# Rearranging the last three tiles of a routed decoder layer: one root for two rows, a sum on TensorE, norms on VectorE

## What is computed

```python
logits = x @ Wr + br
probs = softmax(logits)
top_w, top_idx = top_k(probs, 1)
h = silu(x @ Wg[e]) * (x @ Wu[e])      # D_FF = 1024, e = top_idx
y = h @ Wd[e]
x = layernorm(x + y * top_w)           # over the 256 columns, eps = 1e-5
```

## Time and profile before

| what | us |
|---|---|
| median of 3 runs | 197.69 |
| lowest and highest of them | 196.77, 198.11 |
| span of the profiled execution, first to last instruction | 194.3 |
| TensorE busy in it | 176.0 (91%) |
| VectorE busy | 132.0 (68%) |
| ScalarE busy | 103.3 (53%) |
| GpSimd busy | 103.0 (53%) |
| mean granted TensorE clock | 0.980 of full |

### The profile page before, as it was taken

One profiled execution on the slowest core, in us unless ns is written; L12 is line 12 of the kernel. 1 busy time (PEld: TensorE's weight loads), 2 busy tenths in 40 slices (PEclk: granted clock), 3 DMA queues, 4 the chain that ended last, 5 costly groups with the idle time before them and its releaser, 6 DMA issues.

```text
span 194.3 us, 3905 instructions
## 1 busy us (share of the span) xinstructions
PE 176.0 (91%) x969; PEld 140.0 (72%) x969; DVE 132.0 (68%) x406; ACT 103.3 (53%) x274; POOL 103.0 (53%) x130
## 2 busy tenths in 40 slices
PE   1999997999999898989999999999999999999810
PEld 0677775447888655668888788888888888888610
DVE  3269996895678887536554454444799986888950
ACT  3136776725567935537664946643665422455530
POOL 7006356770126884627772168860588810377683
PEclk9999999999999999999999999999999999999975
DMA  5999999246999223146544105444050000011010
GB/s 157 359 336 418 378 366 319 73 139 168 322 334 405 101 85 94 29 130 173 221 149 150 46 0 165 164 162 167 0 162 3 0 0 3 0 57 56 22 62 24
DMA packets 15317, 29.14 MB, mean 150 GB/s; under 512 B 1726, under 2 KB 11968, under 8 KB 15170
## 3 DMA queue, kind: packets, MB, share of 16 engines
q1 hardware_dynamic: 13568, 25.68, 39.4%
q0 software_dynamic: 1440, 3.22, 4.7%
q10 hardware_dynamic: 290, 0.01, 0.1%
HBM read 20.41 MB, written 9.28 MB: 153 GB/s over the span
## 4 chain that ended last, share of the span: by engine, by line
PE 68%; POOL 11%; issue 7%; DMA 5%; DVE 3%; ACT 3%; POOLq 1%; SPq 1%; DVEq 0%; ACTq 0%
PE bank L484 14%; PE bank L486 13%; PE bank L485 13%; POOL out_tokens L473 5%; PE bank L729 4%; PE bank L563 4%; PE bank L652 3%; PE bank L629 3%; POOL rstd L395 3%; DMA arena<-in_attn_w 3%; PE bank L594 2%; PE bank L572 2%; PE bank L511 2%; DMA x_sorted<-buf,slot 1%; PE bank L498 1%
## 5 line engine op out<-in xcount | busy, mean ns | idle before, releaser
L391 POOL TENSOR_TENSOR w_lo<-stage,w_hi 128x512 fp32r<-128x512 f32 x40 | 51.4, 1305 | 44.0 <-ACT w_hi L803 44.0
L912 ACT ACTIVATE gate<-bank 128x256 f32<-128x256 f32 x44 | 17.0, 387 | 48.5 <-PE bank L486 48.5
L1206 DVE TENSOR_TENSOR hid<-bank,gate 128x256 f32<-128x256 f32 x44 | 18.7, 425 | 30.5 <-ACT gate L912 30.2
L484 PE MATMUL bank<-w_hi,xr 128*128 x88 | 35.9, 408 | 1.4 <-DVE xr L1164 0.8
L486 PE MATMUL bank<-w_hi,xr 128*128 x88 | 34.7, 395 | 0.0
L485 PE MATMUL bank<-w_lo,xr 128*128 x88 | 34.7, 394 | 0.0
L484 PE MATMUL bank<-w_hi,hT 128*128 x88 | 28.5, 324 | 0.7 <-DVE hT L1211 0.7
L803 ACT ACTIVATE w_hi<-stage 128x512 fp32r<-128x512 f32 x48 | 28.6, 630 | 0.3 <-PE bank L486 0.3
L486 PE MATMUL bank<-w_hi,hT 128*128 x88 | 24.9, 282 | 0.0
L485 PE MATMUL bank<-w_lo,hT 128*128 x88 | 24.8, 282 | 0.0
L484 PEld LDWEIGHTS bank<-w_hi,xr 128*128 128x128 f32 x88 | 16.6, 189 | 4.4 <-issue 2.3
(11 more groups left out here) (182 smaller groups left out, 329.7 us busy)
## 6 DMA issues: line engine op xcount, KB each, us to landing
stage<-in_w_ffn SPq DMA_DIRECT2D x16, 768.0 KB, 4.5
rows<-x_sorted SPq DMA_DIRECT2D x22, 132.0 KB, 2.3
x_sorted<-padrow SPq DMA_DIRECT2D x1, 2244.0 KB, 10.2
x_sorted<-padrow SPq DMA_DIRECT2D x1, 2112.0 KB, 16.4
buf<-in_x_tok SPq DMA_DIRECT2D x1, 1024.0 KB, 11.0
w_hi<-in_ctx SPq DMA_DIRECT2D x1, 1024.0 KB, 11.5
w_hi<-in_ctxT SPq DMA_DIRECT2D x1, 1024.0 KB, 14.0
x_sorted<-padrow SPq DMA_DIRECT2D x1, 792.0 KB, 12.7
```

What stands on the lines that cost most here:

```text
L391: g.tensor_tensor(out=lo, in0=src, in1=hi.bitcast(F32), op=ALU.subtract).then_inc(split_lo, 1)
L484: mm(dst, xhi, whi, start=start, stop=False)
L912: a(gate[:, (T + j) % 2, :], fA[j % 2][:, 0:FQ], ACT.Silu).then_inc(silu_done, 1)
L1206: v.tensor_tensor(out=hid[:, (T + j) % 2, :], in0=fA[j % 2][:, FQ:2 * FQ], in1=gate[:, (T + j) % 2, :], op=ALU.mult).then_inc(h_done, 1)
```

## The change

At the end of the kernel:

- Tile 10's `acc` is formed in the third quarter as `rows*lsum + acc` in place of `acc*topw + rows`, and its last sum is made by TensorE: an identity matmul puts `acc` into the bank ahead of the down products of item 43. VectorE takes the moments of tile 10 straight from the bank (`finish_last`). Since the row is then larger by the factor `lsum`, the eps added to its variance is `eps*lsum^2`, which one more instruction in `gates` makes (`eps_last`).
- GpSimd takes one root of two columns for tiles 9 and 10 (`last_roots`). It stands behind store 7 and ahead of store 8.
- The norms of tiles 9 and 10 are made by VectorE in one instruction each (`norm_direct`), and no longer by ScalarE.
- In the last steps VectorE makes the low part of item 43 ahead of the moments of tile 8. For tiles 1 to 7 `finish_norm(t-1)` moves from behind the moments of tile t to just ahead of them.

```diff
--- before.py
+++ after.py
@@ -146,6 +146,8 @@
         lexp = sb("lexp", [P, T, E])
         lsum = sb("lsum", [P, T])
         topw = sb("topw", [P, T])
+        eps_last = sb("eps_last", [P, 1])
+        rstd_last = sb("rstd_last", [P, 2])
 
         reach = rows[:, T - 3, 0:CHUNKS * BLOCKS].rearrange("p (c j) -> p c j", c=CHUNKS)
         has_slot = rows[:, T - 2:T, :].rearrange("p t c -> p (t c)")[:, 0:T * BLOCKS].rearrange("p (t j) -> p t j", t=T)
@@ -229,7 +231,7 @@
         mask_ready, r_done, slot_ready = (sem(n) for n in ("mask_ready", "r_done", "slot_ready"))
         tables, row_table = sem("tables"), sem("row_table")
         lexp_done, topw_ready = sem("lexp_done"), sem("topw_ready")
-        out_ready = sem("out_ready")
+        out_ready, last_added = sem("out_ready"), sem("last_added")
 
 
         LN1, LN3 = 0, CHUNKS
@@ -271,6 +273,7 @@
         CONSTS = 23
 
         items = [(q, t) for q in range(NQ) for t in range(T)]
+        LAST, ITEM_LAST = T - 1, NQ * T - 1
         block = ctx.enter_context(nc.Block())
 
 
@@ -465,14 +468,26 @@
                     if q < NQ - 1:
                         for k in quarter_pieces(q + 1, t):
                             split(k)
-            root(LN3, 0, 0)
-            for t in range(T):
-                if t + 1 < T:
-                    root(LN3 + t + 1, (t + 1) % 2, 0)
+            def root_of(t):
+                root(LN3 + t, t % 2, 0)
+
+            def last_roots():
+                pool.wait_ge(var_ready, LN3 + T)
+                g.tensor_tensor(out=rstd_last[:], in0=mv[:, :, 0, 1], in1=mhalf[:, 0:2], op=ALU.pow).then_inc(rstd_ready, 1)
+
+            def store(t):
                 pool.wait_ge(out_ready, t + 1)
                 g.indirect_dma_start(out=out, out_offset=bass.IndirectOffsetOnAxis(ap=outidx[:, t:t + 1], axis=0),
                                      in_=buf[:, t, 0:D], in_offset=None, bounds_check=TOKENS - 1,
                                      oob_is_err=False).then_inc(d_out, 16)
+
+            root_of(0)
+            for t in range(T - 3):
+                root_of(t + 1)
+                store(t)
+            last_roots()
+            for t in range(T - 3, T):
+                store(t)
 
 
         @block.tensor
@@ -731,15 +746,18 @@
 
             def fdown(j):
                 q, t = items[j]
-                pe.wait_ge(hlo_done, j + 1)
                 if j >= 2:
                     pe.wait_ge(y_read, T + j - 1)
                 b = j % 2
                 off = offs.pop(j)
+                if j == ITEM_LAST:
+                    pe.wait_ge(last_added, 1)
+                    mm(fY[j % 2][:, 0:D], ident[:], acc[:, LAST, :], start=True, stop=False)
+                pe.wait_ge(hlo_done, j + 1)
                 for k in range(FQ // P):
                     w = bass.ds(off + ((q % 2) * E * CHUNK + GU + k * D), D)
                     last = split_mm(fY[j % 2][:, 0:D], hT[:, b, 0, k * P:(k + 1) * P], hT[:, b, 1, k * P:(k + 1) * P],
-                                    w_hi[:, w], w_lo[:, w], k == 0, k == FQ // P - 1)
+                                    w_hi[:, w], w_lo[:, w], k == 0 and j != ITEM_LAST, k == FQ // P - 1)
                 last.then_inc(y_done, 1)
 
             pe.wait_ge(tables, 2)
@@ -937,7 +955,7 @@
                     if 1 <= i <= len(items):
                         fhhi(i - 1)
                 t = i - 4 - (len(items) - T)
-                if t >= 0:
+                if 0 <= t < T - 2:
                     norm_row(t)
                 if i < len(items):
                     q, t = items[i]
@@ -1219,7 +1237,11 @@
                 elif q < NQ - 1:
                     v.tensor_tensor(out=acc[:, t, :], in0=fY[j % 2][:, 0:D], in1=acc[:, t, :],
                                     op=ALU.add).then_inc(y_read, 1)
-                if q == NQ - 2:
+                if q == NQ - 2 and t == LAST:
+                    dve.wait_ge(y_read, T + j + 1)
+                    v.scalar_tensor_tensor(out=acc[:, t, :], in0=rows[:, t, 0:D], scalar=lsum[:, t:t + 1],
+                                           in1=acc[:, t, :], op0=ALU.mult, op1=ALU.add).then_inc(last_added, 1)
+                elif q == NQ - 2:
                     dve.wait_ge(y_read, T + j + 1)
                     step(v.scalar_tensor_tensor(out=acc[:, t, :], in0=acc[:, t, :], scalar=topw[:, t:t + 1],
                                                 in1=rows[:, t, 0:D], op0=ALU.mult, op1=ALU.add))
@@ -1228,18 +1250,35 @@
                 dve.wait_ge(lexp_done, 1)
                 step(v.reduce_sum(lsum[:], lexp[:], AX.X))
                 step(v.reciprocal(topw[:], lsum[:]))
+                step(v.scalar_tensor_tensor(out=eps_last[:], in0=lsum[:, LAST:T], scalar=EPS, in1=lsum[:, LAST:T],
+                                            op0=ALU.mult, op1=ALU.mult))
                 step(v.tensor_copy(outidx[:], rows[:, :, TOK]))
 
-            def finish(t):
+            def finish_sum(t):
 
                 dve.wait_ge(y_done, T + len(items) - T + t + 1)
                 r = buf[:, t, 0:D]
                 v.scalar_tensor_tensor(out=r, in0=fY[(len(items) - T + t) % 2][:, 0:D], scalar=topw[:, t:t + 1],
                                        in1=acc[:, t, :], op0=ALU.mult, op1=ALU.add).then_inc(y_read, 1)
+
+            def finish_moments(t):
                 dve.wait_ge(y_read, len(items) + t + 1)
-                step(v.bn_stats(stats[:, t % 2, :], r))
+                step(v.bn_stats(stats[:, t % 2, :], buf[:, t, 0:D]))
                 step(v.bn_aggr(mv[:, t % 2, 0, :], stats[:, t % 2, :]))
                 variance_eps(t % 2, 0).then_inc(var_ready, 1)
+
+            def finish_last():
+                dve.wait_ge(y_done, T + len(items))
+                step(v.bn_stats(stats[:, LAST % 2, :], fY[ITEM_LAST % 2][:, 0:D]))
+                step(v.bn_aggr(mv[:, LAST % 2, 0, :], stats[:, LAST % 2, :]))
+                v.scalar_tensor_tensor(out=mv[:, LAST % 2, 0, 1:2], in0=mv[:, LAST % 2, 0, 1:2], scalar=eps_last[:],
+                                       in1=ones_f[:, 0:1], op0=ALU.add, op1=ALU.mult).then_inc(var_ready, 1)
+
+            def norm_direct(t):
+                r = fY[ITEM_LAST % 2][:, 0:D] if t == LAST else buf[:, t, 0:D]
+                v.scalar_tensor_tensor(out=buf[:, t, 0:D], in0=r, scalar=mv[:, t % 2, 0, 0:1],
+                                       in1=rstd_last[:, t % 2:t % 2 + 1].broadcast_to([P, D]),
+                                       op0=ALU.subtract, op1=ALU.mult).then_inc(out_ready, 1)
 
             def finish_norm(t):
                 dve.wait_ge(rstd_ready, LN3 + t + 1)
@@ -1248,7 +1287,7 @@
                 v.scalar_tensor_tensor(out=nmr[:, t % 2:t % 2 + 1], in0=mv[:, t % 2, 0, 0:1], scalar=-1.0,
                                        in1=rstd[:, t % 2, 0:1], op0=ALU.mult, op1=ALU.mult).then_inc(nmr_ready, 1)
 
-            for i in range(len(items) + 3):
+            for i in range(len(items) + 1):
                 if i == EARLY:
                     fhlo(i - 1)
                     fxlo(i)
@@ -1259,16 +1298,30 @@
                         fxlo(i + 1)
                     if i < len(items):
                         fhidden(i)
+                    if i == len(items):
+                        finish_sum(T - 3)
+                        finish_norm(T - 4)
                     if 1 <= i <= len(items):
                         fhlo(i - 1)
                 if 2 <= i <= len(items) + 1 - T:
                     fsum(i - 2)
                 if i == T + 1:
                     gates()
-                if i - 2 >= 3 * T and i - 2 < len(items):
-                    finish(i - 2 - 3 * T)
-                if i - 3 >= 3 * T:
-                    finish_norm(i - 3 - 3 * T)
+                t = i - 2 - 3 * T
+                if 0 <= t < T - 3:
+                    finish_sum(t)
+                    if t >= 1:
+                        finish_norm(t - 1)
+                    finish_moments(t)
+            finish_moments(T - 3)
+            finish_sum(T - 2)
+            finish_moments(T - 2)
+            finish_norm(T - 3)
+            finish_last()
+            dve.wait_ge(rstd_ready, LN3 + T - 1)
+            dve.wait_ge(out_ready, T - 2)
+            norm_direct(T - 2)
+            norm_direct(T - 1)
 
 
 def kernel(**inputs):
```

## The result

The changed kernel took 198.52 us (median of 16 runs, 197.16 to 199.5) against 197.26 for the kernel before (16 runs, 196.1 to 198.15), measured side by side: ratio 1.0062, interval 1.0037 to 1.0087, so 1.2 us slower (0.7 to 1.7). The profiled execution has a span of 196.7 us, 2.4 more than that of before.

A forecast was written before the change was run, and what follows sets the result against it. TensorE was taken to bound the kernel, with GpSimd carrying the chain in the last 10 us. -0.3 at the end and +0.68 in gates gave +0.38 on 197.69, 198.07, stated as 198.0; range 196.8 to 198.9.

The forecast's parts named there:

- the collision in gates: VectorE's added eps instruction waits for GpSimd's first split, the cast for the second, delaying TensorE: cost 0.68 us.
- a gain at the end: Last stores on GpSimd: store 10 starts earlier by 0.38 us, taken as 0.3; bounds -0.06 and about 0.7.
- (A): The forecast case: both the gain at the end and the collision in gates, 197.9 to 198.2; chance 58%.
- nothing behind takes it up: TensorE after gates: the 0.68 us delay of item 12's products passes on in full.
- store 8 beside VectorE's norms: GpSimd's end: a VectorE norm overlapping store 8 stretches it by 0.1 us, at most 0.44.
- The low part of item 43: VectorE's end: needing only ScalarE's copy, it starts at about 183.28 instead of 183.93, 0.65 us earlier.
- The identity product: TensorE before item 43's products: 0.60 us, inside the 0.71 us wait for the low part, so costing nothing.
- the place of that root, the cost I named: GpSimd's end: stores 8 to 10 stand behind the double root's wait; store 8 starts at 187.55 instead of 187.28.
- (B): In gates the cast gets in at the border or splits fall otherwise; only the end counts: 197.4, to 197.0; 27%.
- (C): The end gives nothing or loses, store 8 waiting for tile 10's moments and stretched; with the collision 198.4; 10%.
- (D): The identity product misses its gap or the new order stalls TensorE elsewhere, up to 1 us more: 199; 5%.

The follow-up runs named there:

- experiment 2: The kernel before with only the one-column eps instruction added in gates, its result unused; ratio 1.0091 to the kernel before.
- experiment 3: The kernel before with a one-column, one-input reciprocal added in gates, its result unused; ratio 1.0010 to the kernel before.
- experiment 8: The kernel of experiment 6 with the down product's waits in their old order (low part, then bank) except for the last item; ratio 0.9963 to the kernel before.
- experiment 6: The changed kernel with eps moved out of gates to iteration 34 and TensorE's weight offset loaded early, ahead of the waits; ratio 0.9967 to the kernel before.
- experiment 10: The changed kernel, eps still in gates, with the weight offset loaded early; ratio 1.0010 to the kernel before.
- experiment 7: The changed kernel with eps moved out of gates and store 8 issued ahead of the double root; ratio 1.0066 to the kernel before.
- experiment 9: The kernel before with only the weight offset loaded early; ratio 0.9983 to the kernel before.
- experiment 1: The changed kernel with its eps instruction moved out of gates to iteration 34; ratio 1.0022 to the kernel before.

## Why the prediction was right, and where its sizes were off

The forecast was slower, by the collision in gates against a gain at the end, +0.38 in all. The sign and both mechanisms held; measured were +1.26 in the medians and +1.11 in the landmarks. The time, 198.52, lies in the range given, but that says little for the sizes: the range, 196.8 to 198.9, would have held a gain of the end alone as well. The forecast's base, 197.69 from three runs, was also 0.43 above the 197.26 of the sixteen, which made the miss of the time (0.5) smaller than that of the rise, which is three times the forecast. The time lies outside (A)'s own 197.9 to 198.2. And I had put what can be told from no change at 2 us; with sixteen runs of each kernel the interval of the rise is 0.7 to 1.7, clear of 0.

**The collision, forecast 0.68, measured 1.22.** Each part of its chain came as written: the new instruction about 0.65 (0.66), the cast about 1.2 (1.23), both ending with a split. Experiments 2 and 3 show that it is this and not the instruction's length or its wait. By the Trainium skill, "SBUF — State Buffer", section "SBUF: two separate sides", a VectorE instruction with two SBUF inputs and a GpSimd one that reads SBUF exclude each other from a shared port pair, which each holds for its whole length. The eps rows agree (0.66 for one column), and the reciprocal, which runs in 0.17 beside the split, marks the other side of the rule. The down product of item 12 moved by 0.78 where 0.68 was forecast; the 0.1 between is the changed order of waits (experiment 8), and with the old order, in experiment 2, it moved by 0.66. The term that was missing is the 0.41 to 0.44 behind it, the open load of the next offset (experiments 6 and 10). The step that fell short is "nothing behind takes it up", which put everything behind the down product at 0: I had looked for slack that would take the delay away, and not for work that the delay uncovers, here 0.41 to 0.44 us. The trace of before showed the pattern once, an idle of 0.18 with releaser "issue" right behind a late down product, and I had cited that row only as proof that TensorE is full.

**The end, forecast -0.30, measured -0.14.** From root 8 on the forecast was 2.14 to the double root, 0.72 for it, 0.18 to store 8, 1.14 for it, and 0.30 + 0.98 + 0.30 to store 10; measured are 2.16, 0.73, 0.20, 1.23, 0.31 + 0.97 + 0.30. The largest miss is store 8 beside VectorE's norms: stretched by 0.19 where I took 0.1, between my bounds of 0 and 0.44. The low part of item 43, 0.65 earlier, came exactly (1.37 behind hidden 43, where it was 2.02). The identity product, 0.59, did not lie in an idle of TensorE, which the earlier low part had all but used up: it starts at 186.29, right behind the down products of item 42 and 0.03 after the low part of item 43 ends (185.84 + 0.42 = 186.26), so it holds up item 43's products, which start at 186.53. By the 0.14 from low part to product of the kernel before that is about 0.13, an estimate. It cost nothing at the end, since VectorE never waited for the bank: item 43's last matmul starts at 187.31 and the moments at 188.28. The double root waited for VectorE's variance, as written, and the place of that root, the cost I named, is the better one by 1.19 (experiment 7).

**The rivals.** (B), the cast slipping in, did not happen in any of the three profiles with the eps instruction there (1.23, 1.23 and 1.22). (C), the end losing, did not either: in all eight kernels with the changed end and the root first, root 8 to store 10 is 5.82 to 5.90, against 6.04 in the kernels with the old one. (D) had put a further stall of TensorE at 5%; the size of the miss is of its kind, though its place is the offset and not the identity product.

## What to carry to other kernels

An instruction's price is not its length but what it shares and what it uncovers: before adding even one column of work on VectorE, look which GpSimd instruction runs beside it, and give it the form or the place that does not meet it. When a queue that runs full is made to wait once, look at what follows the wait in that queue, above all register loads: here one cost nothing visible in nearly every item but 0.41 to 0.44 us behind a wait, and moving it in front of the wait gave 0.41 to 0.43 us in experiments 6, 9 and 10, with the wait itself left in place. And to judge edits smaller than the scatter of whole runs, measure between landmarks inside the profile that enclose the edit, and keep the ratio as the final word on sign.

## What was not expected of the hardware

- A one-column instruction cost 1.1 us of a 196 us kernel (1.08 between the landmarks of experiment 2), some seven times the 0.15 that it takes by itself.
- A cast of 11 columns with a single tensor input waits for a GpSimd split just as the two-input form does (0.66, 0.47 and 1.23, each ending with a split, and 0.17 with no split near), while a reciprocal and a sum of the same size do not.
- An indirect DMA on GpSimd takes 1.04 after a root, 0.97 behind another store, and 1.23 or 1.16 beside VectorE norms with two or one SBUF inputs; it was stretched, never blocked for the norm's length.
- The regular item of the last layer took 2.33 us in some profiles and 2.30 in others of nearly the same code (hidden 15 to 16 in experiments 1 and 3), and from hidden 15 to hidden 43 it was 65.67 and 65.16, 0.5 us apart; together with the 2.9 us over which hidden 0 scatters, this is larger than most effects studied here.
